# An FFN stream of seven matmuls in every step beside attention, value products last, and divisions on another engine

## What is computed

```
xn = layernorm(x)                                     # 4 x 512 x 512
q, k, v = xn @ Wq, xn @ Wk, xn @ Wv                   # 32 heads of 16; 8 groups of k and v, 4 heads share one
attn = softmax(q k^T / 4)                             # 512 x 512 per head
s = (attn @ v) @ Wo
up, gate = H(xn) @ W_up^T, H(xn) @ W_gate^T           # 2048 each; H is a Hadamard transform with signs
g = silu( H(silu(gate) * up) @ W_down^T )             # with scales
x = x + s * g
```

## Time and profile before

| | us |
|---|---|
| median of 3 runs | 1599.25 |
| the runs | 1598.33 to 1602.5 |
| the profiled execution, its own time | 1601.76 |
| its span, first to last instruction | 1600.0 |
| PE busy | 1373.1 (86%) |
| DVE busy | 1163.4 (73%) |
| ACT busy | 716.2 (45%) |
| POOL busy | 471.6 (29%) |
| first layer, up to the end of its last residual | 793.1 |

### The profile page before, as it was taken

One profiled execution on the slowest core, in us unless ns is written; L12 is line 12 of the kernel. 1 busy time (PEld: TensorE's weight loads), 2 busy tenths in 40 slices (PEclk: granted clock), 3 DMA queues, 4 the chain that ended last, 5 costly groups with the idle time before them and its releaser, 6 DMA issues.

```text
span 1600.0 us, 24278 instructions
## 1 busy us (share of the span) xinstructions
PE 1373.1 (86%) x8972; PEld 670.0 (42%) x8972; DVE 1163.4 (73%) x1937; ACT 716.2 (45%) x1253; POOL 471.6 (29%) x387
## 2 busy tenths in 40 slices
PE   3777799999999999999729888998799888898887
PEld 1222233333333333333315437654475535744365
DVE  6788888787877887885166777587675796666944
ACT  2453466556655665565056412364035431354221
POOL 1229931012201220121104523165122642135331
PEclk9998899999999999999958999999999999999999
DMA  4411000010000000000180221101300113002021
GB/s 147 186 53 47 1 8 8 14 34 14 7 21 27 15 7 21 28 20 1 60 329 1 51 38 43 34 17 41 79 15 27 31 21 80 26 16 51 14 40 40
DMA packets 78996, 68.50 MB, mean 43 GB/s; under 512 B 45888, under 2 KB 67104, under 8 KB 76832
## 3 DMA queue, kind: packets, MB, share of 16 engines
q1 hardware_dynamic: 78880, 66.96, 13.9%
HBM read 44.87 MB, written 17.87 MB: 39 GB/s over the span
## 4 chain that ended last, share of the span: by engine, by line
PE 22%; DVE 18%; DMA 4%; ACT 3%; issue 2%; POOL 1%; SPq 0%; DVEq 0%; ACTq 0%; POOLq 0%
PE abank L1915 5%; DVE tok L1555 3%; PE vbank L1967 3%; PE fbank L1931 2%; PE vbank L2026 2%; PE vbank L2134 2%; PE vbank L2162 1%; PE abank L2041 1%; PE abank L2154 1%; DVE tok L1563 1%; DVE tok L1557 1%; DVE tok L1574 1%; DMA big<-t_scratch 1%; DMA t_scratch<-tok 1%; POOL big L1351 1%
## 5 line engine op out<-in xcount | busy, mean ns | idle before, releaser
L481 DVE TENSOR_REDUCE mS<-bank 128x1 f16<-128x512 f32 x512 | 328.9, 685 | 102.8 <-PE bank L844 102.0
L689 ACT ACTIVATE probs<-bank 128x512 f16<-128x512 f32 x512 | 277.2, 594 | 178.0 <-PE bank L851 177.9
L898 PE MATMUL bank<-xnT,ug_hi 128*128 128x512 f16 x512 | 195.1, 381 | 0.1
L898 PE MATMUL bank<-xnT,ug_lo 128*128 128x512 f16 x512 | 194.0, 379 | 0.0
L321 POOL TENSOR_TENSOR h<-th,h 128x512 f16<-128x512 f32 x58 | 68.1, 1175 | 271.0 <-ACT h L660 271.0
L1947 PE MATMUL fbank<-down,hid 128*128 128x512 f16 x512 | 124.0, 406 | 24.3 <-DVE hid L1473 24.3
L844 PE MATMUL bank<-ks,qs 32*128 32x512 f16 x512 | 101.6, 393 | 30.5 <-issue 7.2
L1931 PE MATMUL fbank<-xT,up 128*128 128x512 f16 x512 | 118.6, 386 | 4.7 <-ACT hid L1747 4.7
L1915 PE MATMUL abank<-xT,w 128*128 128x512 f16 (+1 forms) x480 | 115.8, 393 | 6.5 <-DVE w L1421 6.5
L851 PE MATMUL bank<-qB,ks 32*128 32x512 f16 x512 | 100.4, 389 | 0.0
L912 PE MATMUL bank<-dn,h 128*128 128x512 f16 x256 | 98.0, 383 | 0.0
(11 more groups left out here) (280 smaller groups left out, 2693.4 us busy)
## 6 DMA issues: line engine op xcount, KB each, us to landing
h<-in_ug SPq DMA_DIRECT2D x8, 1024.0 KB, 5.0
lt_scratch<-big SPq DMA_DIRECT2D x16, 384.0 KB, 2.7
dn<-in_down SPq DMA_DIRECT2D x2, 2048.0 KB, 9.4
x_scratch<-th SPq DMA_DIRECT2D x16, 256.0 KB, 2.0
hid<-in_upw SPq DMA_DIRECT2D x2, 2048.0 KB, 13.9
res<-x_scratch SPq DMA_DIRECT2D x16, 256.0 KB, 3.4
out_x<-res SPq DMA_DIRECT2D x16, 256.0 KB, 2.0
big<-in_w SPq DMA_DIRECT2D x2, 1548.0 KB, 10.6
```

The costliest lines, as they stand in the source:

```text
L481: v.tensor_reduce(mS[:, u % 2, qt, 32 * j + DH:32 * j + DH + 1], SA[n % 2][:, :], AX.X, ALU.max).then_inc(S["max_done"], 1)
L689: a.activation(probs[:, n % (2 * G), :], SB[n % 2][:, :], ACT.Exp, scale=float(DH) ** -0.5).then_inc(S["p_ready"], 1)
L898: mm = pe.matmul(GB[n % 2][:, :], w[:, kt, col:col + P], xnb(b, kt), start=r == 0, stop=r == 2 * KT - 1)
```

## The change

A function `ffn_stream(t)` lists PE's FFN matmuls of step t. For batch 0 it gives what stood there before, one tile of 8 per step from m = 32. For the later batches it takes one row of 192 down matmuls (4 x 48) and 256 of gate and up (32 x 8) and cuts it into 64 pieces of seven. The steps at which ACT, DVE and POOL take a tile are worked out from it: the step after the one in which the tile ends (`GATE_AT`, `UP_AT`, `DOWN_END`, now 7, 14, 21, 28). The output projections come at steps 14, 17, 22 and 29 instead of 17, 19, 28 and 35. Weigh moves on PE behind the FFN matmuls of its step. On DVE q_aug moves ahead of gate_mul and up_mul. From unit 5 on the multiplication by the reciprocals is POOL's. The numbers of the arithmetic are the same.

```diff
-DOWN_END = (8, 16, 24, 32)
-OUT_STEP = (17, 19, 28, 35)
+OUT_STEP = (14, 17, 22, 29)
+DIVIDE_FIRST = 5
+DOWN_MM, GU_MM = 3 * FT, 2 * KT
+STREAM = TT * DOWN_MM
+PER_STEP = (STREAM + UG * GU_MM) // BSTEPS
+def ffn_stream(t):
+    b, m = t // BSTEPS, t % BSTEPS
+    if b == 0:
+        return [("gu", 0, m - FFN_STEP, r) for r in range(GU_MM)] if m >= FFN_STEP else []
+    work = []
+    for s in range(PER_STEP * m, PER_STEP * (m + 1)):
+        if s < STREAM:
+            n, j = divmod(s, DOWN_MM)
+            work.append(("down", (b - 1) * TT + n, j // 3, j % 3))
+        elif b < B:
+            work.append(("gu", b) + divmod(s - STREAM, GU_MM))
+    return work
+GU_END = {w[1:3]: t for t in range(TEND) for w in ffn_stream(t) if w[0] == "gu" and w[3] == GU_MM - 1}
+GATE_AT = {t + 1: (b, c // 2) for (b, c), t in GU_END.items() if c % 2 == 0}
+UP_AT = {t + 1: (b, c // 2) for (b, c), t in GU_END.items() if c % 2}
+DOWN_END = tuple((DOWN_MM * (n + 1) - 1) // PER_STEP + 1 for n in range(TT))
...
 @block.gpsimd
+            def divide(u):
+                g = u % NKV
+                pool.wait_ge(S["rl_ready"], u + 1)
+                pool.wait_ge(S["o_done"], u)
+                if g % 2 == 0:
+                    pool.wait_ge(S["oT_ready"], u // 2)
+                pool.tensor_tensor(otok[:, :, DH * (g % 2):DH * (g % 2) + DH], oblk[:, :, 0:DH],
+                                   rl[:, :].rearrange("p (c d) -> p c d", d=1).to_broadcast([P, SC, DH]),
+                                   ALU.mult).then_inc(S["o_done"], 1)
...
+                if t in UP_AT and UP_AT[t] >= (0, LOW_FIRST):
+                    low_rows(*UP_AT[t])
+                if t % STEPS == 3 and DIVIDE_FIRST <= t // STEPS - 2 < NU:
+                    divide(t // STEPS - 2)
...
 @block.vector
+                if u > DIVIDE_FIRST:
+                    v.wait_ge(S["o_done"], u)
                 v.reciprocal(rl[:, :].rearrange("p (c d) -> p c d", d=1), oblk[:, :, DH:DH + 1]).then_inc(S["rl_ready"], 1)
+                if u >= DIVIDE_FIRST:
+                    return
...
-                if b < B and m > FFN_STEP and m % 2:
-                    gate_mul(b, (m - FFN_STEP) // 2)
-                if t > FFN_STEP + 1 and (t - 2) // BSTEPS < B and (t - 2) % BSTEPS >= FFN_STEP and t % 2 == 0:
-                    up_mul((t - 2) // BSTEPS, ((t - 2) % BSTEPS - FFN_STEP) // 2)
+                if t % STEPS == 0 and 0 < t <= NU * STEPS:
+                    q_aug(t // STEPS - 1)
+                if t in GATE_AT:
+                    gate_mul(*GATE_AT[t])
+                if t in UP_AT:
+                    up_mul(*UP_AT[t])
...
-                if t % STEPS == 0 and 0 < t <= NU * STEPS:
-                    q_aug(t // STEPS - 1)
...
 @block.tensor
-                if t % 2 and t > LAG and (t - LAG - 2) // 2 < NU * TT:
-                    weigh((t - LAG - 2) // 2)
...
-                for half in range(2):
-                    if b and m < FFN_STEP:
-                        down_mm((b - 1) * TT + m // 8, 2 * (m % 8) + half)
-                    if b < B and m >= FFN_STEP:
-                        for r in range(KT * half, KT * half + KT):
-                            ffn_mm(b, m - FFN_STEP, r)
+                for work in ffn_stream(t):
+                    if work[0] == "down":
+                        down_mm(*work[1:])
+                    else:
+                        ffn_mm(*work[1:])
+                if t % 2 and t > LAG and (t - LAG - 2) // 2 < NU * TT:
+                    weigh((t - LAG - 2) // 2)
```

More of the change, by code:

```diff
@@ L63, in gb_order @@
             order.append(("ug", t - PREP - 2))
-        if b and m < FFN_STEP and m % 8 == 0:
-            order.append(("down", (b - 1) * TT + m // 8))
-        if b < B and m >= FFN_STEP:
-            order.append(("gu", b, m - FFN_STEP))
+        order += [w[:2] for w in ffn_stream(t) if w[0] == "down" and w[2:] == (0, 0)]
+        order += [w[:3] for w in ffn_stream(t) if w[0] == "gu" and w[3] == 0]
     return {k: n for n, k in enumerate(order)}
@@ L337, in _ @@
                 b, m = t // BSTEPS, t % BSTEPS
-                fb, fm = (t - 2) // BSTEPS, (t - 2) % BSTEPS
-                if fb < B and fm >= FFN_STEP and t % 2 == 0 and (fb or (fm - FFN_STEP) // 2 >= LOW_FIRST):
-                    low_rows(fb, (fm - FFN_STEP) // 2)
+                if t in UP_AT and UP_AT[t] >= (0, LOW_FIRST):
+                    low_rows(*UP_AT[t])
+                if t % STEPS == 3 and DIVIDE_FIRST <= t // STEPS - 2 < NU:
+                    divide(t // STEPS - 2)
                 if b and m - 2 in OUT_STEP:
@@ L722, in _ @@
                 b, m = t // BSTEPS, t % BSTEPS
-                if b < B and m > FFN_STEP and m % 2:
-                    tanh_gate(b, (m - FFN_STEP) // 2)
+                if t in GATE_AT:
+                    tanh_gate(*GATE_AT[t])
                 if 0 <= t - LAG < NU * STEPS:
@@ L736, in _ @@
                     high_down(DN_AT.index(t))
-                if t > FFN_STEP + 1 and (t - 2) // BSTEPS < B and (t - 2) % BSTEPS >= FFN_STEP and t % 2 == 0:
-                    high_rows((t - 2) // BSTEPS, ((t - 2) % BSTEPS - FFN_STEP) // 2)
+                if t in UP_AT:
+                    high_rows(*UP_AT[t])
                 if t % 16 == Q_STEP + 1 and t // 16 + 1 < NU // 2:
@@ L900, in ffn_mm, with down_mm @@
                     mm.then_inc(S["gb_full"], 1)
-            def down_mm(n, j):
+            def down_mm(n, j, part):
                 k, ft = GO["down", n], DN_TURN[j]
[L905 to L910, removed]
-                bk, rows = GB[k % 2][:, :], slice(n % TT * P, (n % TT + 1) * P)
-                pe.matmul(bk, h16(ft, 0)[:, rows], dn16(ft, 0), start=j == 0, stop=False)
-                pe.matmul(bk, h16(ft, 0)[:, rows], dn16(ft, 1), start=False, stop=False)
-                mm = pe.matmul(bk, h16(ft, 1)[:, rows], dn16(ft, 0), start=False, stop=j == FT - 1)
-                if j == FT - 1:
+                if part == 0:
+                    if j == 0:
+                        pe.wait_ge(S["gb_took"], k - 1)
+                    if n % TT == 0:
+                        pe.wait_ge(S["row_lo"], n // TT * FT + ft + 1)
+                    if n == 0:
+                        pe.wait_ge(S["mb_took"], MB["dn", j] + 1)
+                mm = pe.matmul(GB[k % 2][:, :], h16(ft, part // 2)[:, n % TT * P:(n % TT + 1) * P], dn16(ft, part % 2),
+                               start=(j, part) == (0, 0), stop=(j, part) == (FT - 1, 2))
+                if (j, part) == (FT - 1, 2):
                     mm.then_inc(S["gb_full"], 1)
```

## The result

| us | before | changed |
|---|---|---|
| median (runs) | 1599.95 (4) | 1669.37 (4) |
| range of the runs | 1598.33 to 1602.5 | 1668.41 to 1671.95 |
| profiled execution | 1601.76 | 1668.41 |
| its span | 1600.0 | 1666.3 |
| first layer, end of its last residual | 793.1 | 859.4 |

The ratio is 1.0435, with a 95% interval of 1.0416 to 1.0454: slower by 69.4 us in the medians and by 66.65 us in the two profiled executions, where 58.7 us were forecast. On the median that is 1669.4 us for a forecast of 1658.

The account below looks back on a forecast made before the run. PE was taken to bound the kernel, nearly always at work, DVE with some room. Batches 1 to 3 +61.2 us, batch 0 -2.5, division and end 0: +58.7, so 1658 us on the median; bounds 1640 to 1672.

Parts of the forecast that it names:

- The stall inside the step: Gate and up tiles starting mid-step wait on PE for DVE's eviction behind the maxima: 28.0 us a batch.
- What bounds it: PE nearly always at work, DVE with some room; a bank cannot be taken before 2.3 us into its step.
- The tile starts inside the step: Gate and up half: five starting positions wait 1.65 to 0.78 us each, 6.08 us a unit, 28.0 us a batch.
- Step 28: Batches 1 to 3: its first gate or up tile waits 1.87 us for DVE to take the last down product.
- The even stream without waits: Seven matmuls a step: a unit of 17.15 us; PE alone would need 146.2 us for batch 2, 8.1 less.
- the signs: Trace marks of a right forecast: batch 174 us, units of 23 us behind step 32, 17 to 19 before.
- Weigh last, qB first: Weigh and scores stop waiting for DVE; in batch 0 worth -2.5 us, between -5 and +1.
- wherever in the step it stands: Odd steps of batches 1 to 3: weigh counted at 0.33 us whatever its place, giving 2.28 us a step.
- Division on POOL: Multiplication by reciprocals moved from DVE takes 0.6 to 1.2 us on POOL, hidden; 0 for both sides.
- The end: Last batch's 192 down matmuls stay PE-bound at 54.1 us with or without the change: 0, within 1 us.
- TensorE's clock: Granted clock left at 1.00 (2.4 GHz) in the sum; the rival that it falls, 1677 us, had chance 0.12.

Follow-up runs that it names:

- take_between: The changed kernel with the gate or up tile taken between the step's first and second row maximum, from batch 1 on: 1644.97 us, ratio 1.0284.
- take_first: The changed kernel with DVE taking the gate or up tile ahead of the step's two row maxima, from batch 1 on: 1606.41 us, ratio 1.0042.
- seven_down_whole_tiles: The changed kernel with only down products seven to a step; gate and up tiles whole, eight matmuls in steps 32 to 63: 1613.95 us, ratio 1.0086.
- the one without them: The changed kernel with evictions ahead of maxima, early tanh and last down tile first, from batch 1 on: 1591.96 us; with weigh in front throughout, 1591.79 us.

## Why the prediction came out right, point by point

The stall inside the step was sized almost exactly, and it carries the sum. The measured 1669.4 us is 11 us over the 1658 forecast, inside the forecast's own bounds of 1640 to 1672 us but near their upper end.

- *What bounds it.* Right. The parts of a step (0.33, 0.216, 0.41, 1.70 us) came back within 0.02 us, and the stalled steps of unit 7 are within 0.05 us of the numbers worked out.
- *The tile starts inside the step.* Right in place, order and size; take_between and take_first show it to be the cause, since they move nothing but the eviction. Step 28, with the last down tile, took 3.77 us for 3.82.
- *The even stream without waits.* Right to 1%, a little short. A projection behind weigh costs about 1.0 us instead of 0.87 (v: 4.66 against 3.66 us for the same step of unit 7), eight times a batch; the scores after a unit's first step wait 0.22 us for ACT's exponentials in every second unit of the gate and up half; and step 24 waits 0.42 us for DVE's product with the output projection (`gated`). Together the batches came out 1.7, 1.3 and 0.7 us longer than worked out. The units in front of step 32 took 18.1, 18.0, 20.2 and 22.1 us, where the signs named 17 to 19: these left out the projections and the stalls of steps 28 to 30, which the sum had.
- *Weigh last, qB first.* The term of the sum that failed. For batch 0 it stood at -2.5 us with bounds of -5 and +1, and the batch ended 1.5 us later (279.4 for 277.8), outside these bounds. I had read only what weigh waits for, not what it covers. In the stalled steps the same error hid in the sum: the 0.33 us "wherever in the step it stands" were right for the changed kernel, but in front they would have cost nothing, so moving weigh was part of the loss, 13 us of 69 (3 us in each of the batches 1 to 3, 4 in batch 0). The sum for the batches 1 to 3 did not suffer by it, since it adds up the changed kernel as it stands; the share of the single edit was wrong, a loss counted as a gain.
- *Division on POOL.* Right: 0.62 us, hidden; alone it changes nothing.
- *The end.* Right, 54.1 us in both.
- *TensorE's clock.* Right to leave it at 1.00: the second half of batch 2, with PE busy 75.95 of 97.00 us, kept 2.4 GHz. Of the rule weighed there (the Trainium skill, TensorE: Matmul & The Clock Gate, "A second HAM failure mode: psum-queue depth-cycling"), that short idles between groups are enough to make the rate swing, the changed kernel shows nothing, though PE idled up to 1.5 us in five steps of eight. The lower rate did come in seven_down_whole_tiles, after a stretch in which PE was busy 0.57 of 2.00 us.

The difference that was missing, 7.95 us between the profiled executions (66.65 for 58.7), is 4.0 us of batch 0, 3.7 us of the batches 1 to 3, and 0.3 us between an execution's own time and its span. The medians lie 69.4 us apart because the profiled execution of the kernel before is 1.8 us over its median and that of the changed kernel 1.0 us under. The profile of before has the longest batch 0 of the seven kernels with weigh in front (248.8 us; the others 245.7 to 246.7), so against a usual one batch 0 lost about 3 to 4 us, not 1.5.

## What to carry to other kernels

When work is cut evenly over steps, ask of each tile where in the step it now starts, and where its bank's eviction stands in the other engine's order in that same step; a ring of "scores, maxima, eviction, rest of the matmuls, scores" costs its whole length, while both engines look idle. First move the eviction ahead (same instructions, 63 us here), and then the operation that feeds it. Before moving an operation out of a gap, read what it hides as well as what it waits for: with the value products in front, the kernel with the long waits was 13 us faster, and the one without them lost 1 us in each of the batches 1 to 3.
